# Attention and expert-choice MoE block: where the low pieces of the first expert's W1 and of b2 are made

## The reference

```python
h = _layernorm(x, axis=-1) * (1 + cb) + sb
x = x + gb * _L0_ffn_ref(h, ...)
# inside: 4096 tokens of 256, 8 experts, each takes its 512 best tokens
logits = xf @ router_w + router_b
scores = jax.nn.softmax(logits, axis=-1)
G, idx = jax.lax.top_k(scores.T, K)
toks = xf[idx]
h1 = jax.nn.relu(jnp.einsum('ekh,ehf->ekf', toks, w1) + b1[:, None, :])
eo = jnp.einsum('ekf,efh->ekh', h1, w2) + b2[:, None, :]
contrib = (eo * G[..., None]).reshape(-1, h)
y = jnp.zeros_like(xf).at[idx.reshape(-1)].add(contrib)
```

## Time and profile before

| | us |
|---|---|
| median of three runs | 1686.77 (1685.7 to 1687.25) |
| the profiled execution, its own time | 1684.82 |
| its span | 1683.0 |
| PE busy | 1631.7 (97%) |
| VectorE (DVE) busy | 1462.5 (87%) |
| ScalarE (ACT) busy | 1358.1 (81%) |
| GpSimd (POOL) busy | 254.7 (15%) |

### The profile page before, as it was taken

How to read it: one execution, slowest core, us unless ns; L and a number is a source line. 1 busy time by engine, 2 the same in 40 slices (tenths; PEclk the granted TensorE clock), 3 DMA queues, 4 the chain that set the end, 5 groups by cost and what they waited for, 6 DMA issues and landing times. The chain is left out here.

```text
span 1683.0 us, 44154 instructions
## 1 busy us (share of the span) xinstructions
PE 1631.7 (97%) x17243; PEld 935.8 (56%) x17243; DVE 1462.5 (87%) x2913; ACT 1358.1 (81%) x2640; POOL 254.7 (15%) x323
## 2 busy tenths in 40 slices
PE   7999999999999999999999999999999997599998
PEld 5645555455555555455555555545555585388887
DVE  5678999999999999999999999999999396777773
ACT  2327999999999999999999999999999825365563
POOL 0444222100010000001000000100000012144533
PEclk9999999999999999999999999999999996699999
DMA  8771635222232233223222333332220332235432
GB/s 270 218 225 65 154 75 112 48 47 49 54 68 45 47 63 55 49 47 71 53 45 46 52 58 58 66 53 49 49 45 13 113 125 73 98 89 138 114 66 35
DMA packets 101276, 134.44 MB, mean 80 GB/s; under 512 B 27164, under 2 KB 73820, under 8 KB 97964
## 3 DMA queue, kind: packets, MB, share of 16 engines
q1 hardware_dynamic: 90444, 115.33, 30.0%
q0 software_dynamic: 7808, 14.68, 3.9%
q10 hardware_dynamic: 2816, 1.61, 0.4%
HBM read 89.64 MB, written 40.63 MB: 77 GB/s over the span
## 5 line engine op out<-in xcount | busy, mean ns | idle before, releaser
L1215 ACT ACTIVATE pt<-ps 128x512 f32<-128x512 f32 x2048 | 1074.9, 606 | 66.0 <-PE ps L699 48.9
L1238 DVE TENSOR_REDUCE pmax<-ps 128x1 f32<-128x512 f32 x1626 | 1006.7, 682 | 51.2 <-PE ps L1300 50.6
L699 PE MATMUL ps<-qp,kp 50*128 50x512 f32 x2048 | 706.7, 446 | 0.7 <-ACT pt L1215 0.5
L1300 PE MATMUL ps<-kp,qp 48*128 48x512 f32 x1812 | 635.6, 448 | 0.1
L1318 PE MATMUL ps<-pt,v_st 128*32 128x256 f32 (+1 forms) x10752 | 589.6, 335 | 0.7 <-ACT pt L1215 0.7
L1300 PEld LDWEIGHTS ps<-kp,qp 48*128 48x128 f32 x1812 | 294.1, 184 | 222.0 <-DVE pmax L1238 128.0
L699 PEld LDWEIGHTS ps<-qp,kp 50*128 50x128 f32 x2048 | 330.8, 184 | 132.6 <-ACT pt L1215 115.9
L1318 PEld LDWEIGHTS ps<-pt,v_st 128*32 128x32 f32 x10752 | 265.5, 109 | 245.4 <-issue 175.2
L291 POOL CAST m_parts<-rowmax_t 128x32 fp32r<-128x32 f32 x64 | 13.4, 210 | 776.8 <-DVE rowmax_t L323 776.8
L1242 DVE CUSTOM_DVE_ANT_0 stage_b<-ps,stage_b 128x512 f32<-128x512 f32 x186 | 126.3, 679 | 0.3 <-issue 0.3
L1201 ACT ACTIVATE stage_b<-ps 128x512 f32<-128x512 f32 x186 | 114.3, 614 | 0.0
(11 more groups left out here) (243 smaller groups left out, 1496.1 us busy)
## 6 DMA issues: line engine op xcount, KB each, us to landing
kp<-k_parts SPq DMA_DIRECT2D x186, 128.0 KB, 4.5
v_all<-L_ffn_w SPq DMA_DIRECT2D x16, 1024.0 KB, 6.3
qp<-q_parts SPq DMA_DIRECT2D x186, 64.0 KB, 4.0
k_parts<-pt SPq DMA_DIRECT2D x16, 512.0 KB, 4.2
q_parts<-pt SPq DMA_DIRECT2D x16, 512.0 KB, 3.1
o_rows<-o_sb SPq DMA_DIRECT2D x64, 128.0 KB, 3.6
sums_c<-o_rows SPq DMA_DIRECT2D x512, 0.5 KB
kd<-kd_parts SPq DMA_DIRECT2D x186, 32.0 KB, 1.8
```

Source lines behind the costliest of these rows:

```text
L699: nc.tensor.matmul(bank(n % SCORE_BANKS), kp[rows, h % NBUF, kt * P:(kt + 1) * P], qp[rows, h % NBUF, f * CH:(f + 1) * CH], start=True, st ...
L1215: nc.scalar.activation(pt[:, s % PTS, half * CH:(half + 1) * CH], bank(n % SCORE_BANKS), ACT.Exp, scale=SCALE).then_inc(scores_out, 1)
L1238: v.reduce_max(pmax[:, u % 2, at:at + 1], part_slot(n), AX.X).then_inc(groups_out, 1)
L1300: mm(part_slot(n), qp[rows, r, col:col + P], keys, start=True, stop=True).then_inc(groups_full, 1)
```

## The change

The subtraction that makes the low pieces of the first expert's W1 goes from VectorE's list in the expert block to GpSimd's in the search block, between the constants and the splitting of the scores. The semaphore `gather_issued` is dropped. The subtraction for b2 goes behind the low pieces of the first expert's tokens and of its W2. For the other seven experts nothing changes.

```diff
--- before.py
+++ after.py
@@ -1450,6 +1450,9 @@
                     g.tensor_tensor(weights[:, 0, :], weights[:, 0, :], weights_2[:, 0, :], ALU.add)
                     g.tensor_tensor(weights[:, 1, :], weights[:, 1, :], weights_2[:, 1, :], ALU.mult)
 
+                    pool.wait_ge(w1_high, 1)
+                    g.tensor_tensor(w1_l[:], w1_sb[0], w1_h.bitcast(F32), ALU.subtract).then_inc(w1_low, 1)
+
                     pool.wait_ge(score_done, 1)
                     link(g.tensor_copy(score_e[:], logits[:].rearrange("p t e -> p e t")))
                     for i in range(SPLIT):
@@ -1653,7 +1656,7 @@
             hid_f = [pair.rearrange("p (f t) -> p f t", f=2) for pair in (stage_b[:, 1, 0:2 * CAP], spare[:, 0:2 * CAP])]
             rows_in = [sem(f"rows_in{p}") for p in range(2)]
             gather_set, scatter_set, added = sem("gather_set"), sem("scatter_set"), sem("added")
-            gather_issued, second_made = sem("gather_issued"), sem("second_made")
+            second_made = sem("second_made")
             tok_turned, tok_out, hid_out = sem("tok_turned"), sem("tok_out"), sem("hid_out")
             tok_high, w2_high, w2_low = sem("tok_high"), sem("w2_high"), sem("w2_low")
             hid_high, hid_low = sem("hid_high"), sem("hid_low")
@@ -1697,7 +1700,6 @@
                                 contrib[:, cc, :], None, compute_op=ALU.add).then_inc(added, 16)
 
                     gather(0)
-                    pool.sem_inc(gather_issued, 1)
                     for e in range(E):
                         if e + 1 < E:
                             gather(e + 1)
@@ -1837,12 +1839,10 @@
                         make_one_hot(0, g8)
                     v.tensor_scalar(share[:], ident[:], 0.0, 1.0 / HALF, ALU.mult, ALU.add).then_inc(share_set, 1)
                     take_list(0)
-                    dve.wait_ge(gather_issued, 1)
-                    take_w1_low(dve, 0)
+                    take_tokens_low(0)
+                    take_w2_low(0)
                     dve.wait_ge(b2_high, 1)
                     v.tensor_tensor(b2_p[HALF:P], b2_row[HALF:P], b2_p[HALF:P].bitcast(F32), ALU.subtract).then_inc(b2_done, 1)
-                    take_tokens_low(0)
-                    take_w2_low(0)
                     for e in range(last_e):
                         place_values(e + 1)
                         for g8 in range(4):
```

## The result

| | before | changed |
|---|---|---|
| median of nine runs, us | 1686.77 | 1694.45 |
| lowest to highest | 1684.27 to 1689.5 | 1691.57 to 1700.7 |
| ratio, 95% interval | | 1.0045 (1.0025 to 1.0066) |
| span of the profiled execution | 1683.0 | 1692.3 |
| GpSimd busy | 254.7 | 257.5 |

The change makes the kernel slower, by 4.2 to 11.1 us with the interval's ends; the forecast was 1692.6, in a range of 1688.0 to 1695.6.

A forecast was written before the change was run, and what follows sets the result against it. The prediction took VectorE to bound the search and the expert block's start until 1468.53, then PE's matmuls. Its terms, +4.3 - 0.85 + 2.3 = +5.8 us on 1686.8, gave 1692.6 us, range 1688.0 to 1695.6.

The forecast's parts named there:

- The search, +4.3: Search block: VectorE's CAST of line 1519 waits for GpSimd's 4.5 us subtraction and the COPY behind it, +4.3 us.
- follows without a gap: Search block: GpSimd's 0.64 us COPY directly follows its subtraction, so VectorE gets in only after both.
- +3.7: Search block: variant by the literal lock rule, VectorE released between GpSimd's subtraction and its COPY, +3.7 us instead of +4.3.
- The gathers, -0.85: Expert block's start: gathers freed of VectorE's ops land earlier, so PE turns the rows when its spare matmuls end, -0.85 us.
- b2, +2.3: Expert block: b2's subtraction ahead of the second expert's one-hot tiles lengthens PE's wait to some 4.7 us, +2.3 us.
- The half-clock stretch, 0 ± 1.4: Expert block: PE's slow stretch behind its wait for the one-hot tile may move or lengthen, counted 0 with ±1.4 us.
- W1 of the third expert, 0: Expert block: its 1 MB load starts at the block's start, not beside the gathers, and leaves their transfers alone, zero.
- The sum, +5.8: Whole kernel: search, gathers and b2 terms together, +4.3 - 0.85 + 2.3 = +5.8 us.
- Not held: Search-block rival: GpSimd's subtraction runs beside the CAST and digit rounds, no measurable change, 1.4 us, 1688.2; chance 0.18.
- Only the two-input ops are held: Search-block rival: the CAST passes, line 1533 waits, +2.7 us in the search, +4.1 in all, 1690.9; chance 0.10.
- The gathers are not freed by VectorE: Expert-block rival: the load or queue stretches the gathers, so the 0.85 us is not gained, 1693.5; chance 0.06.

The follow-up runs named there:

- e2: Against the changed kernel, b2's subtraction back ahead of the tokens' low pieces, so only W1's subtraction is moved to GpSimd; ratio 0.9998 to the kernel before.
- e1: Against the kernel before, only b2's subtraction moved; W1's low piece still made by VectorE beside the gathers; ratio 1.0007.
- e8: As e6, but VectorE's W1 and b2 subtractions in four pieces each and only the second expert's first one-hot tile ahead; ratio 0.9969 to the kernel before.
- e3: Against the changed kernel, GpSimd's subtraction moved behind its splitting of the scores; ratio 1.0031 to the kernel before.
- e5: Against the changed kernel, GpSimd's subtraction split into eight pieces of 128x256 in the same place; ratio 1.0014 to the kernel before.
- e7: Against the kernel before, W1's subtraction moved to GpSimd behind its four gathers, b2 left in place; ratio 0.9984.
- e4: Against the kernel before, the first expert's W2 low pieces put ahead of the tokens' low pieces; ratio 0.9961, median 1683.45 us against 1688.73.
- e11: As e8, with 24 spare matmuls on PE ahead of the turning instead of 28; ratio 1.0000 to the kernel before.
- e0: The change run and profiled once more, unaltered; ratio 1.0032 to the kernel before.
- e9: Against the kernel before, 32 spare matmuls on PE ahead of the turning instead of 28; ratio 0.9996.
- e10: e6 run once more with more rounds; ratio 0.9996 to the kernel before.
- e6: As e4, with the second expert's placing and first two one-hot tiles also ahead of the tokens' low pieces; ratio 0.9969 to the kernel before.

## Why the prediction was right

- **The search, +4.3: measured +3.9** (44.78 in both profiles of the change and 44.74 in e2, against 40.86). The mechanism was the one named: the CAST of line 1519 held by GpSimd's subtraction. Its length was right (4.5 forecast, 4.53 measured). The step that missed is that GpSimd's COPY "follows without a gap": VectorE got in before the COPY. The rule of the Trainium skill (SBUF — State Buffer, Who interferes with whom), read literally, gave +3.7 and was nearer. Line 1493, on which I had leaned against it, showed again its 1.85 us behind three GpSimd instructions, so both orders occur.
- **The gathers, -0.85: measured -0.27 in the change's first profile and -1.03 in its second.** VectorE did hold them (e1, e2, e8), and PE's filler did set the turning. But the 28 spare matmuls are no fixed 8.36 us: they took 7.68 to 9.27 in the profiles, by when the clock rose from 0.50 within them. The row of one execution was taken for a constant. The first gather took 1.13 us, not 0.95, as it had before.
- **b2, +2.3: measured +2.45.** The wait is 4.93 us against 4.7 forecast. Nothing covers it (e1).
- **The half-clock stretch, 0 ± 1.4: measured 0.0** in the change (11.63 against 11.62) and -0.3 in its second profile, though with W1 alone on GpSimd it was -1.5 (e2).
- **W1 of the third expert, 0: measured 0 on the path.** But the earlier load did not leave the gathers' transfers alone: the slowest landed 2.9 us after its start instead of 6.0, and only 1.0 us of the difference was its wait for VectorE. PE's filler hid this.
- **The sum, +5.8: measured +6.1 and +5.1** in the two profiles; by run times +4.2 to +11.1 and +2.5 to +8.4. That it comes so near is in part luck: in the first profile the search fell 0.4 us short and the gathers 0.6 us, with opposite signs. And the median's +7.7 holds the spread of the search block's start, for which the prediction has no term.
- **The rivals.** "Not held" is refuted by the CAST's 4.15 us. "Only the two-input ops are held" is refuted by the same row, and e3 shows that those are held as well. "The gathers are not freed by VectorE" is refuted by e1, and the inference of the Trainium skill (same page and section) that a tensor_tensor does not hold up descriptor generation does not hold for these gathers: the VectorE ops beside them were all TENSOR_TENSORs with both inputs in SBUF.

## What to carry to other kernels

GpSimd's idle time is no free time: a long GpSimd instruction beside a chain of small VectorE instructions cost the chain nearly its full length at both places tried (the change, e3), and 1.6 instead of 3.9 us in eight pieces (e5). Put such work where VectorE waits for something else (e7), or use that wait for VectorE's own work: moving one call ahead of another (e4) gave 5.3 us by the medians (3.4 to 9.6 by the interval), 2.35 by its profile. Before moving a step behind another, look which of the two engines is waiting for the other there; b2's subtraction cost at most the 0.86 us that PE idled while it stood beside the gathers, and its whole length two steps later.

## What the runs showed of the hardware that was not expected

An indirect DMA on GpSimd was held by VectorE's running TENSOR_TENSOR at its start and then took some 0.85 us: 2.48 us in e2, ending 0.85 us after the VectorE op; the two pieces of e8 give the same to 0.03 us. The first gather of the kernel before began 0.02 us ahead of VectorE's op and took its 1.13 us, as in the change, where no op stood beside it. So it is at its start that a gather is held.

The granted clock rose within the same 28 matmuls at different times from one execution to the next (7.68 to 9.27 us for the lot), and this alone moved the turning by 0.8 us.

PE's half-clock stretch behind the rows' turning, which costs 1.2 to 2.4 us, was there when PE had idled 0.86, 0.70, 0.50 and 1.97 us before the turning (before, e4, e7, e11), and when it waited 4.8 to 4.9 us for the one-hot tile (the change, e0, e1, e3, e5). It was absent with no idle time before the turning and a wait of 2.4 us or none (e2, e8, e9, e10), but also in e6, with 1.72 us of idle time. What decides in e6 stays open, and so does what spreads the start of the search block from 1400.9 to 1406.6.
